# Fused attention and expert layer on one core: where SyncE issues the expert weights within a chunk of the attention

## The reference, cut to what matters

```
qkv, qkv_a = ln(x) @ Wqkv + b, ctx @ Wqkv_aux + b_aux
p, pa      = softmax(q k' / sqrt(8)), softmax(q ka' / sqrt(8))      # 16 heads of width 8
out        = (p v)(1 - gate) + (pa va) gate
x          = x + tanh(g_xattn) (out @ Wo + bo)
w_dense    = top-8 of sigmoid(ln(x) @ gate_w'), in groups, normalised, x 2.5
y          = sum over 64 experts of w_dense (silu(h We_gate) * (h We_up)) We_down
x          = x + tanh(g_ffn) (y + shared expert)
```

## Time and profile before

| what | value |
|---|---|
| median of three runs | 871.06 us |
| the profiled execution's own time | 874.03 us |
| its span, first to last instruction | 872.2 us |
| PE busy | 832.4 us (95%) |
| DVE, POOL, ACT busy | 690.8, 637.7, 565.8 us |
| granted clock of TensorE | full, all through |
| DMA | 125.27 MB, mean 144 GB/s |

### The profile page before, as it was taken

One profiled execution on the slowest core, in us unless ns is written; L12 is line 12 of the kernel. 1 busy time (PEld: TensorE's weight loads), 2 busy tenths in 40 slices (PEclk: granted clock), 3 DMA queues, 4 the chain that ended last, 5 costly groups with the idle time before them and its releaser, 6 DMA issues.

```text
span 872.2 us, 20170 instructions
## 1 busy us (share of the span) xinstructions
PE 832.4 (95%) x6733; PEld 646.8 (74%) x6733; DVE 690.8 (79%) x1656; ACT 565.8 (65%) x964; POOL 637.7 (73%) x602
## 2 busy tenths in 40 slices
PE   5899999998898889999999999999999999999997
PEld 3467777776675668888888888887888888888885
DVE  6789899998888858778777877967976977877655
ACT  4377888887777756566566567548557556656554
POOL 2476888887883357887787786887787788778785
PEclk9999999999999999999999999999999999999999
DMA  5567777777653156646554654654746555655552
GB/s 131 175 173 188 182 192 189 186 193 182 168 156 81 32 138 151 151 119 148 134 134 123 168 133 109 169 129 110 179 119 143 145 134 126 148 131 140 143 137 58
DMA packets 113747, 125.27 MB, mean 144 GB/s; under 512 B 28000, under 2 KB 76064, under 8 KB 112208
## 3 DMA queue, kind: packets, MB, share of 16 engines
q1 hardware_dynamic: 110768, 123.47, 56.8%
q10 hardware_dynamic: 2880, 0.59, 0.4%
HBM read 103.55 MB, written 19.96 MB: 142 GB/s over the span
## 4 chain that ended last, share of the span: by engine, by line
PE 75%; DMA 6%; DVE 2%; issue 2%; ACT 2%; POOL 1%; SPq 0%; DVEq 0%; ACTq 0%; POOLq 0%
PE bank L1963 20%; PE bank L1965 20%; PE bank L1964 20%; PE bank L1305 4%; DMA stack_q<-nmaxT 3%; PE bank L1292 3%; PE bank L1279 2%; DMA stack_k<-k_scratch 1%; PE bank L1261 1%; PE bank L1249 1%; DMA cwb<-wts_scratch 1%; ACT prob L787 1%; PE bank L1313 1%; PE bank L1940 1%; PE bank L1326 1%
## 5 line engine op out<-in xcount | busy, mean ns | idle before, releaser
L1640 POOL TENSOR_TENSOR hid<-act,cwb 128x512 f32<-128x512 f32 x264 | 424.4, 1616 | 125.7 <-DVE act L1867 71.7
L1693 ACT ACTIVATE silu<-bank 128x512 f32<-128x512 f32 x256 | 152.8, 597 | 193.7 <-PE bank L1965 189.2
L1867 DVE TENSOR_TENSOR act<-silu,bank 128x512 f32<-128x512 f32 (+1 forms) x264 | 180.5, 684 | 118.8 <-ACT silu L1693 76.6
L1963 PE MATMUL bank<-xhi,weights_hi 128*128 128x512 f32 x520 | 206.7, 397 | 0.4 <-ACT silu L1693 0.4
L1875 DVE TENSOR_TENSOR hlo<-hid,hhi 128x512 fp32r<-128x512 f32 x256 | 199.4, 779 | 7.3 <-ACT hhi L1699 7.0
L1965 PE MATMUL bank<-xlo,weights_hi 128*128 128x512 f32 x520 | 204.1, 392 | 0.0
L1964 PE MATMUL bank<-xhi,weights_lo 128*128 128x512 f32 x520 | 203.8, 392 | 0.0
L984 DVE TENSOR_REDUCE mx<-bank 128x4 f32<-128x512 f32 x256 | 167.5, 686 | 22.4 <-PE bank L1279 18.7
L1699 ACT ACTIVATE hhi<-hid 128x512 fp32r<-128x512 f32 (+1 forms) x264 | 165.0, 625 | 13.3 <-POOL hid L1640 10.9
L787 ACT ACTIVATE prob<-bank 128x1024 f32<-128x1024 f32 x128 | 131.0, 1024 | 64.0 <-PE bank L1292 61.8
L1965 PEld LDWEIGHTS bank<-xlo,weights_hi 128*128 128x128 f32 x520 | 97.6, 188 | 22.0
(11 more groups left out here) (235 smaller groups left out, 1003.0 us busy)
## 6 DMA issues: line engine op xcount, KB each, us to landing
cwb<-wts_scratch SPq DMA_DIRECT2D x174, 384.0 KB, 5.4
stack_k<-k_scratch SPq DMA_DIRECT2D x30, 384.0 KB
k_scratch<-parts_k SPq DMA_DIRECT2D x15, 384.0 KB, 3.3
stack_q<-q_scratch SPq DMA_DIRECT2D x30, 192.0 KB
k_scratch<-parts_k SPq DMA_DIRECT2D x15, 256.0 KB, 3.9
q_scratch<-parts_q SPq DMA_DIRECT2D x15, 192.0 KB, 2.2
xin<-in_x_dram SPq DMA_DIRECT2D x16, 128.0 KB, 2.5
cin<-in_ctx_dram SPq DMA_DIRECT2D x16, 128.0 KB, 2.6
```

The lines of the kernel that those rows point to most:

```text
L1640: pool.tensor_tensor(h_buf[k][:], a_buf[k][:], cwb[slot][:, q % GP, :], ALU.mult).then_inc(h_ok, 1)
L1693: act.activation(s_buf[k % RS][:], g_bank[k % 2][:], ACT.Silu).then_inc(s_ok, 1)
L1867: nc.vector.tensor_tensor(a_buf[k % RS][at], s_buf[k % RS][at], u_bank[k % 3][at], ALU.mult).then_inc(a_ok, 1)
L1963: nc.tensor.matmul(bank, w[0], mh, start=first, stop=False)
```

## The change

Two edits. In SyncE's `body` the call of `expert_weights` moves from ahead of `load_stack_k` to behind `load_stack_k` and `store_x2`. And the first group holds ten experts in place of eight, so that the last holds four in place of six; the groups between keep ten. The wait of ScalarE follows from the same constant: pair 4 is now in the first group, and pair 5, half a chunk later, is the first that needs the second.

```diff
-    FIRST_E = E // LOOPS
+    FIRST_E = EACH_E
     LAST_E = E - FIRST_E - EACH_E * (LOOPS - 3)
...
                     load_stack_q(n + 2)
                     store_k(n + 2, i)
-                if g < LOOPS - 2:
-                    expert_weights(g, j)
                 if not last:
                     load_stack_k(n + 2)
                 if n > 0:
                     store_x2(n - 1, 1 - j)
+                if g < LOOPS - 2:
+                    expert_weights(g, j)
```

## The result

The change makes the kernel slower: 889.75 us in the median of four runs (885.13 to 895.01), before 871.33 in four; the ratio is 1.020, 95% interval 1.016 to 1.024. The prediction said 868.6 us, a range of 865.5 to 873.8, and "faster" as the likeliest. It was wrong in sign, and outside even what its slower rival allowed.

What follows compares the result with a forecast made beforehand. PE bounds even chunks; later ones lose time to PE's waits for shift transfers and a late key stack. Terms -5.1 + 1.5 + 1.1 = -2.5 us, from 871.06 to 868.6 us; the 8-in-10 range is 865.5 to 873.8.

Steps and rivals of the forecast that it cites:

- slower rival: The late q store delays k store, key stack and PE: 875 us, range 872.8 to 877, chance 0.25.
- The key-stack load isn't issued earlier: SyncE's key-stack load goes out once the k store lands; moving weights brings 0 in even chunks, up to 0.6 us late.
- The three shift waits go: PE's three waits for ScalarE's 16 KB shift transfer in chunks with weights vanish, a gain of 4.1 us.
- The q store behind the weights: On SyncE's queue the q store lands 1.7 us later; key stack moves 0 to 0.6 us, 1.1 us in all.
- slack of 1.6: Microseconds to spare on SyncE between the stack_q load's issue and the k store's, nearly all used up by the delay.
- the prediction's 252 GB/s: Rate of the busiest 2 us around there, by which 480 KB of weights take 1.9 us.
- The price per chunk: Key stack's later issue: 0.12 us for each of nine even chunks, bounds 0 and 0.5 us each.
- The first group: ScalarE waits at its first weights near 74 us, once: 1.5 us, bounds 0 and 2.
- the later of the forecast's two times, 76.3: First group's landing if 1.9 us behind the residual's store, which lands at 74.4; the earlier time was 74.8.
- Rival C: q store behind weights delays k store, key stack and PE if key stack issues over 0.3 us after shift; 875 us, chance 0.25.

Runs made afterwards that it cites:

- k_store_first: Against the change: the k store issued ahead of the stack_q load in each chunk; 891.35 us, ratio 1.021.
- down_behind: Against the change: only the 160 KB of down weights behind the residual's store, from chunk 2 on, other weights in the old place; 873.68 us, ratio 0.999.
- light_weights: Against the change: from the second group on each weight load brings two experts in place of ten, with as many DMAs; 878.44 us, ratio 1.006.
- loads_q_weights: Against the change: next token loads, then q store, then weights, all behind the residual's store and ahead of the stack_q load; 878.33 us, ratio 1.007.
- behind_q_store: Against the change: the weights moved behind the next q store, directly ahead of the next token loads; 898.98 us, ratio 1.031.
- token_loads_early: Against the change: a chunk's token loads issued ahead of the weights, behind the residual's store; 897.40 us, ratio 1.028.
- stack_k_4k: Against the kernel before: each half of the key-stack load cut in two DMAs, packets of 4 KB in place of 8; 873.43 us, ratio 1.000.
- first_ten_only: Against the kernel before: ten experts in the first group, the weights in their old place; 873.53 us, ratio 1.000.

## Why the prediction was wrong, by its own steps

- *The key-stack load isn't issued earlier*: right, and it goes out later still: the k store lands after 4.2 us, not 3.8.
- *The three shift waits go*: right. From 190 to 300 us PE has no wait for a shift transfer. That gain of about 4 us is in the trace and is buried. The weights' place alone doesn't give it: in k_store_first, with the weights in the same place, such waits came to 12.6 us.
- *The q store behind the weights* is the step that failed. The prediction made it 1.7 us later against a slack of 1.6, and so priced it at 0.12 us a chunk. In the chunk shown, the time from the q store's first issue to the stack_q load went from 2.4 to 5.9 us, 3.5 later. 2.3 of this is the landing (4.4 for 2.1): by size a delay of the whole 480 KB (1.9 us at the prediction's 252 GB/s) and a little more. The other 1.1 is SyncE's own issue, 1.50 us for 0.36, a term the sum didn't have at all; it came in five of nine chunks. A slip made it smaller too: 165.46 + 5.9 is 171.4, not 171.0, so by the prediction's own terms the queue was busy to 173.3 and the slack already overdrawn by some 0.3 us. 3.5 less the slack of 1.6 is 1.9 us, and the k store was 2.0 us late. Its landing adds 0.8 and the key stack goes out 2.9 us later in its chain than before. down_behind agrees with the slack, light_weights shows that it is the bytes, and loads_q_weights that it is the place.
- *The token loads* weren't in the sum either. They stood right behind the q store in the chunk of the earlier trace rows, and the prediction named nowhere what they delay. With them directly behind the weights and the q store free, behind_q_store took 898.98 us; with them free and the q store late, token_loads_early took 897.40.
- *The price per chunk* was bounded at 0.5 us, from the chunks after 190 us that had slow q stores. Those had the weights in the k store's bubble and longer chunks already; they were no bound for a q store 3.5 us late. The measured pace is 1.3 us above 16.0.
- *The first group*: 1.5 us, with bounds 0 and 2; ScalarE waited 2.5 and PE 2.2. Chunk 3 took 4.8 us more than before, of which 1.5 are PE's work at the lower clock. The weights' last DMA of that group was issued at 69.43 and landed 7.3 us later, 0.4 us beyond the later of the forecast's two times, 76.3. So the landing was nearly right; what followed the wait was not counted.
- *Rival C* was the right mechanism, at the right place and with the right deciding point (the key stack went out 1.35 us after the shift transfer at 171.12, and PE waited 1.4 us), with a price of 875 us where 889.75 came. Its chance of 0.25 rests on a delay of 1.7 us held against a slack of 1.6 as if both were exact to a tenth.

## What to carry to other kernels

A DMA without a deadline isn't free to go anywhere in a hand-written queue: it needs a gap in which nothing urgent is behind it. In the kernel before, 480 KB stood between the k store and the load that waits for its landing, and that load went out as soon as the store had landed. To price a move, go through every transfer that now stands behind the moved bytes until the queue has drained, take its consumer, and hold the whole delay (bytes, backlog that is already there, and the issuing engine's own time) against that consumer's slack. Where two chains have little slack, test a kernel that frees both; freeing one at a time gave nothing back here (897.40 and 898.98 us for 889.75), freeing both gave back 11 us.

## What the runs showed of the hardware

- *An issue can take longer when much was issued just before.* With the change the same store of 192 KB took SyncE 1.2 to 2.2 us to issue in the five chunks where the issue of 480 KB of weights had ended 0.4 to 1.2 us earlier, and 0.36 us in the four where it had ended 1.5 us earlier or more. With 256 KB more ahead (token_loads_early) the hold-up moved to the down weights' own issue, 2.7 to 4.2 us, and the store took 0.6. With a fifth of the bytes (light_weights) the store took 0.36 in every chunk from 100 us on; the weights' issue had ended 1.9 us earlier or more there.
- *A small transfer on another queue is only as fast as what it meets.* ScalarE's 16 KB landed after 6.3 us behind a key stack in the kernel before, and after up to 8.0 us behind stack_q load and key stack together (k_store_first). The Trainium skill ("DMA: Bandwidth & Descriptors", queues, rings and completion order) has the engines alternate between rings packet by packet; the runs agree in so far as with packets of 4 KB in place of 8 the waits for shift transfers fell from 5.6 to 0.5 us (stack_k_4k), while those for the key stack rose from 1.0 to 2.7 and the time stayed the same.
- *TensorE's granted clock* went to half, 1.2 GHz, for three stretches of 3.4 us or a little more in the attention after the change, each behind a wait of PE of 1.0 to 2.2 us. In the kernel before, with waits of up to 1.5 us from chunk 2 on, none came. PE's busy time in the three chunks rose by 4.8 us. The mean over an execution says little about such stretches. An execution of the kernel before at a mean granted clock of 0.986 took 869.8 us, another at 1.0 took 874.3. Neither has a kept trace, but first_ten_only does, with a mean of 0.985 and 873.53 us: its clock was low mostly in the first two chunks (0.59 and 0.89 of full), and in the first of them PE was busy for 14.5 of 20.0 us only.
